# Two attention blocks with their rounds written out instead of looped, on all engines

## What is computed

```python
def reference(x, ctx_4096, mask_BxSxS2_ff1, ...):
    ...
    # _L0_attn_ref: q, k, v = x @ W.T + b, 32 heads of 16
    scores = jnp.where(causal, jnp.einsum('bhqd,bhkd->bhqk', q, k) / math.sqrt(hd), -jnp.inf)
    out = jnp.einsum('bhqk,bhkd->bhqd', jax.nn.softmax(scores, axis=-1), v)
    ...
    # _L0_xattn_ref: q from x, k and v from the context, q and k rotated (_rope), 4 query heads on each key head
    scores = jnp.einsum('bhgqd,bhkd->bhgqk', qg, k) / scale
    masked = jnp.where(mask[:, None, None].astype(bool), scores, -1000000000.0)
    out = jnp.einsum('bhgqk,bhkd->bhgqd', jax.nn.softmax(masked, axis=-1), v)
    ...
    x = _layernorm(x + _L0_attn_ref(...)); x = _layernorm(x + _L0_xattn_ref(...)); x = _layernorm(x + _L0_ffn_ref(...))
```

## Time and profile before

| | us |
|---|---|
| median of 3 runs | 1984.65 (1984.55 to 1985.22) |
| the profiled execution, whole | 1981.03 |
| its span in the profile | 1979.2 |
| PE busy | 1751.4 (88%) |
| DVE busy | 1353.7 (68%) |
| ACT busy | 940.9 (48%) |
| POOL busy | 936.9 (47%) |

### The profile page before, as it was taken

One profiled execution on the slowest core, in us unless ns is written; L12 is line 12 of the kernel. 1 busy time (PEld: TensorE's weight loads), 2 busy tenths in 40 slices (PEclk: granted clock), 3 DMA queues, 4 the chain that ended last, 5 costly groups with the idle time before them and its releaser, 6 DMA issues. The chain is left out here.

```text
span 1979.2 us, 45274 instructions
## 1 busy us (share of the span) xinstructions
PE 1751.4 (88%) x15496; PEld 1004.4 (51%) x15497; DVE 1353.7 (68%) x2069; ACT 940.9 (48%) x1565; POOL 936.9 (47%) x905
## 2 busy tenths in 40 slices
PE   6999999899999999999999999964678999999910
PEld 4666776555555555555555555533234554555500
DVE  5777888778788788887878888776753333333357
ACT  4556557654555654645545555434222333333334
POOL 6732024564554554645645546514344454445432
PEclk9999999999999999999999999986889999999965
DMA  9520011112221121221312203121313454643369
GB/s 265 124 44 24 3 56 50 54 65 76 75 90 61 65 97 54 97 78 41 118 44 85 86 33 118 65 72 54 106 64 129 141 205 168 220 151 111 111 235 311
DMA packets 82510, 200.13 MB, mean 101 GB/s; under 512 B 8704, under 2 KB 28544, under 8 KB 80320
## 3 DMA queue, kind: packets, MB, share of 16 engines
q1 hardware_dynamic: 63456, 136.89, 20.4%
q0 software_dynamic: 18912, 61.09, 9.9%
HBM read 141.86 MB, written 56.10 MB: 100 GB/s over the span
## 5 line engine op out<-in xcount | busy, mean ns | idle before, releaser
L382 PE MATMUL bank<-xhl,front_h 128*128 128x512 f16 x704 | 270.2, 384 | 20.5 <-DVEq L68 13.1
L383 PE MATMUL bank<-xhl,front_h 128*128 128x512 f16 x704 | 270.2, 384 | 0.0
L384 PE MATMUL bank<-xhl,front_l 128*128 128x512 f16 x704 | 269.9, 383 | 0.0
L1067 POOL TENSOR_TENSOR xa_xs<-xa_xs,sn 128x512 f32<-128x512 f32 x160 | 233.5, 1459 | 59.2 <-ACT xa_xs L1110 59.1
L1072 POOL TENSOR_TENSOR xa_rr<-xa_x,xa_xs 128x512 f32<-128x512 f32 x160 | 232.1, 1450 | 34.0 <-POOL xa_xs L1067 24.0
L1075 POOL TENSOR_TENSOR xa_sc<-xa_sc,xa_rs 128x1024 f32<-128x1024 f32 x32 | 62.2, 1945 | 374.2 <-DVE xa_rs L1281 374.2
L382 PE MATMUL bank<-out_h,xa_oh 128*128 128x512 f16 x512 | 194.2, 379 | 7.4 <-DVE xa_ol L1186 7.3
L383 PE MATMUL bank<-out_l,xa_oh 128*128 128x512 f16 x512 | 194.0, 379 | 0.0
L384 PE MATMUL bank<-out_h,xa_ol 128*128 128x512 f16 x512 | 194.0, 379 | 0.0
L1201 DVE TENSOR_TENSOR xa_x<-bank,cs 128x512 f32<-128x512 f32 x160 | 109.9, 688 | 84.7 <-ACT xa_xs L1110 82.5
L1109 ACT ACTIVATE xa_xs<-bank 64x512 f32<-64x512 f32 x160 | 95.0, 593 | 130.8 <-PE bank L384 127.2
(11 more groups left out here) (308 smaller groups left out, 4929.2 us busy)
## 6 DMA issues: line engine op xcount, KB each, us to landing
xa_rawc<-in_ew SPq DMA_DIRECT2D x33, 768.0 KB, 5.0
moe_ring<-scratch_w SPq DMA_DIRECT2D x16, 1536.0 KB
co_rows<-scratch_y SPq DMA_DIRECT2D x20, 1024.0 KB, 7.7
scratch_w<-xa_chunk_h SPq DMA_DIRECT2D x32, 384.0 KB, 2.3
scratch_w<-xa_chunk_l SPq DMA_DIRECT2D x32, 384.0 KB, 3.1
raw_front<-in_xwq SPq DMA_DIRECT2D x9, 1024.0 KB, 7.2
raw_out<-in_xwo SPq DMA_DIRECT2D x9, 1024.0 KB, 5.2
out<-raw_front SPq DMA_DIRECT2D x17, 256.0 KB, 6.7
```

The source lines that it names most:

```text
L382: pe.matmul(out_ap, ah, bh, start=start and m == 0, stop=False)
L383: pe.matmul(out_ap, ah, bl, start=False, stop=False)
L384: mm = pe.matmul(out_ap, al, bh, start=False, stop=stop and m == n - 1)
L1067: PO.mark(pool.tensor_tensor(xr, xr, sn[:, :].rearrange("p (a s) -> p a s", a=1) .to_broadcast([P, QT // S, S]), ALU.mult), f"sm{r}", st)
```

## The change

Every loop over rounds in `self_attention` and `cross_attention` becomes a Python `range`, on SP, ACT, DVE, PE and POOL. The round number is a constant everywhere, each instruction of each round stands in the program by itself, and no branch is left in the two blocks. What each step does and its order do not change: the steps of the round that was written out already keep their flag (`last`, `first`).

```diff
--- self_attention, sync
-                    with sp.Fori(0, NG - 1) as i:
+                    for i in range(NG - 1):
                         front_weights(i + 1)
--- self_attention, scalar, vector and tensor (the same on each)
-                    with act.Fori(0, NG - 1) as i:
+                    for i in range(NG):
                         for q in range(NQ):
-                            step(i, q)
-                    for q in range(NQ):
-                        step(NG - 1, q, True)
+                            step(i, q, i == NG - 1)
--- cross_attention, sync
-                    with sp.Fori(0, NG) as i:
+                    for i in range(NG):
                         nxt = (i + 1) % NG
--- cross_attention, gpsimd, scalar, vector and tensor (the same on each)
-                    for q in range(NQ):
-                        step(0, q, True)
-                    with pool.Fori(1, NG) as i:
+                    for i in range(NG):
                         for q in range(NQ):
-                            step(i, q)
+                            step(i, q, i == 0)
```

More of the change, by code:

```diff
@@ L791, in step @@
                             DV.mark(dve.scalar_tensor_tensor(wo_l, raw_o, WS, wo_h, ALU.mult, ALU.subtract), "wol", st)
-                    with dve.Fori(0, NG - 1) as i:
+                    for i in range(NG):
                         for q in range(NQ):
-                            step(i, q)
-                    for q in range(NQ):
-                        step(NG - 1, q, True)
+                            step(i, q, i == NG - 1)
                     done = Step(None, 0)
@@ L927, in step @@
                         back_out(st)
-                    with pe.Fori(0, NG - 1) as i:
+                    for i in range(NG):
                         for q in range(NQ):
-                            step(i, q)
-                    for q in range(NQ):
-                        step(NG - 1, q, True)
+                            step(i, q, i == NG - 1)
                     done = Step(None, 0)
@@ L1160, in step @@
                         AC.mark(act.activation(chunk_h[:, :], rawc[:, :], ACT.Copy, scale=WS), "ch", st)
-                    for q in range(NQ):
-                        step(0, q, True)
-                    with act.Fori(1, NG) as i:
+                    for i in range(NG):
                         for q in range(NQ):
-                            step(i, q)
+                            step(i, q, i == 0)
                     back_p(Step(None, 0))
@@ L1285, in step @@
                         DV.mark(dve.scalar_tensor_tensor(chunk_l[:, :], rawc[:, :], WS, chunk_h[:, :], ALU.mult, ALU.subtract), "cl", st)
-                    for q in range(NQ):
-                        step(0, q, True)
-                    with dve.Fori(1, NG) as i:
+                    for i in range(NG):
                         for q in range(NQ):
-                            step(i, q)
+                            step(i, q, i == 0)
                     st = Step(None, 0)
@@ L1385, in step @@
                             back_out(st, (2, 3))
-                    for q in range(NQ):
-                        step(0, q, True)
-                    with pe.Fori(1, NG) as i:
+                    for i in range(NG):
                         for q in range(NQ):
-                            step(i, q)
+                            step(i, q, i == 0)
                     st = Step(None, 0)
```

## The result

The changed kernel takes 1965.62 us (median of 6 runs, 1958.69 to 1968.51) beside 1984.54 us of the kernel before in the same session (6 runs, 1980.39 to 1985.22): a ratio of 0.9902, 95% interval 0.9881 to 0.9922, 18.9 us faster. A second timing gave 1965.3 beside 1984.06 us, 0.9907 (0.9889 to 0.9924).

A forecast was written before the change was run, and what follows sets the result against it. PE (TensorE) was taken to bound both blocks. Self-attention's 9.5 us (5.6 + 2.75 + 1.1) and cross-attention's 1.9 make 11.4 us, from a median of 1984.65 to 1973.2 us; range 1969 to 1979 us.

The forecast's parts named there:

- The bound, the branch, the stall: Both blocks: PE sets the pace; its taken branches back leave it idle, 5.6 us in self-attention and 3.9 at cross-attention's six edges.
- the edges: Passages from one looped round to the next: two in self-attention, six in cross-attention, the latter six predicted to give 1.7 us.
- The rival of the cheap branch: Both blocks: idle time is a wait for DVE and stays; only 1.1 us come back, 1983.5 us; chance 0.07.
- that of the fetches: DVE, ACT and POOL must fetch written-out code every round: 3.8 more blocks, 18.1 us cost, 1991.3 us; chance 0.04.
- the register instructions: Self-attention: constants instead of registers save 0.11 us in each of 10 looped steps, 1.1 us, between 0 and 2.5.
- what follows the stall: Self-attention: the steps behind the two edges are 2.2 and 0.55 us too long, from slow clock and restarting engines; 2.75 us.
- the rest of that row, seven waits of some 0.65 us, ... hangs on ACT and DVE, which are busy throughout, and stays: Cross-attention: PE's waits in each round's second step, behind the split of the output weights, were to gain nothing.
- what the gap loses, the sum itself gives back: Cross-attention, POOL: the 0.15 us shorter gap between product and sum leaves the period equal; the chain gains only 0.2 us.
- the lateness behind an edge: Cross-attention: DVE comes late into the next round, costing PE 0.56 us an edge without any branch, 0.36 after the change.
- the whole stall comes back: Both blocks: POOL's and DVE's chains shorten enough to return all stall time, 15.2 us, 1969.4 us; chance 0.12.
- DVE takes over: Both blocks: PE's gains beyond its own idle time are lost, the clock falls anyway; 6.1 us, 1978.5 us; chance 0.17.

## Why the prediction was right, and where it was wrong

**The bound, the branch, the stall: right.** PE sets the pace, the idle times at the edges are the branch's and not a wait for DVE. With PE looped they are there (2.86 and 2.97 us), without they are gone in every trace. The rival of the cheap branch falls. So does that of the fetches. It counted 3.8 blocks more, and there are 18 fetches more in q14; yet in the profiled execution PE has no idle time without a releaser in the blocks. Over the ten traces with self-attention written out on PE it has 0 to 1.6 us of it there, at no regular distance, against 0 to 1.05 us in the four with the loop.

**Self-attention, 9.5 us predicted, 9.2 measured as a mean and 9.6 in the profiled pair: the sum right, its split wrong.** The stall and what follows it were to give 8.35 us. PE's loop written out alone gives 5.7, or 7.3 without the idle times that nobody releases: the 5.6 of the stalls and the 1.7 of the clock. All engines but PE, on top of that, give 3.9 (183.07 - 179.14), or 2.3 without the same idle times, where the register instructions were to give 1.1. 7.3 and 2.3 are the pair's 9.6. Two errors cancelled.
- The term "what follows the stall" (2.75 us) was too large by 1.05. Of the steps behind the edges, 0.5 us each were put down to engines that start again in sequence; with the same stalls and those engines written out the steps take 17.89 and 17.88 us. The other 1.7 us, the clock's, came in three of four executions with these stalls, and at either edge; no run shows what decides it.
- The term "the register instructions" (1.1 us) was too small by 1.2. Its price of 0.11 us was taken from step (2, 3) alone; the steps (1, 0) and (1, 1) took 0.3 (the clock's 1.7 taken off) and 0.5 us longer than in the changed kernel. Only some 0.4 us of it were hidden by the stalls, in the two steps that end in one (with PE alone written out they take 18.22, without an idle time of 0.16, and 17.99 us, against 17.90).

**Cross-attention, 1.9 us predicted, 7.4 measured: wrong, and in two steps.** By step times the gain (7.6 us in the pair of profiled executions) consists of 3.4 us in seven second steps (30.86 to 30.38), 3.6 in the six last steps (182.3 in all, against 6 x 29.79 = 178.7), 0.3 behind the edges and 0.3 in step (1, 0).
- The step that failed first is "the rest of that row, seven waits of some 0.65 us, ... hangs on ACT and DVE, which are busy throughout, and stays". It was the largest row of the waits, and I set it aside from the names in it. ACT and DVE looped again cost 0.3 us; POOL looped again costs 5.4.
- The step behind it, which mis-sized the edges, is "what the gap loses, the sum itself gives back", from the equal periods of the earlier trace rows. They stand where the sum is contended, and the period there is still 2.90 us in the changed kernel. But the chain to PE goes through the sum's end, and in the chain's first rotations, where nothing contends, the period falls with the gap (1087.00 - 1084.42 = 2.58 us from sum to sum, against 1100.95 - 1098.23 = 2.72), the gaps add up, and DVE is held less long. So the lateness behind an edge did not go from 0.56 to 0.36 us; it went to nothing, and the full 3.9 us of the edges came back.

The rival "the whole stall comes back" had cross-attention's edges right and left out the second steps too; it got 4.35 us for the block. The range ended at 1969 because of it, so both the forecast and the range rested on the one sentence that the second steps stay. The rival "DVE takes over" has a true core: with PE alone written out DVE's lateness costs 0.49 us an edge. The change as made removes it, 0.36 us of it on POOL, as first steps of 30.15 us show with POOL alone looped.

**The rest.** Some 2 us of the measured gain lie outside the blocks, in stages that wander as much between executions of one kernel. They are left as chance; no run rules out a part of them.

## What to carry to other kernels

Time that is lost behind a stall need not be the stall's: put the stall back alone and look whether it returns. A small cost per step is to be read from all steps, not from the one that lies nearest to the control. Where two engines contend, equal periods say nothing; follow the end of the operation that the next engine is released by. And the largest row of waits on the bounding engine is to be traced to the engine that moves it, by its chain back, before it is said to stay.

## What the runs showed of the hardware

- An operation of DVE with two SBUF operands ended 0.54 to 0.55 us after the end of POOL's concurrent sum in four kernels, with durations of 0.76, 0.90, 1.04 and 1.04 us. Two gaps on POOL, each 0.14 us longer, became 0.28 us of DVE's duration.
- The busy time of DVE rose from 1353.7 to 1377.9 us with the same 2,069 operations. With POOL looped, or delayed by the small operation, it stays at 1354.1 and 1354.5. The group of the query's low parts in cross-attention shows it; before and after, from 449 to 1289 us:

```profile
L1206 DVE TENSOR_TENSOR xa_rql<-xa_rr,xa_rqh 128x512 f16<-128x512 f32 x110 | 97.5, 886 | 9.2 <-ACT xa_rqh L1116 7.5
```

```profile
L1196 DVE TENSOR_TENSOR xa_rql<-xa_rr,xa_rqh 128x512 f16<-128x512 f32 x112 | 129.1, 1153 | 7.5 <-ACT xa_rqh L1108 7.0
```

  The mean goes from 886 to 1153 ns while the block gets shorter: part of a busy time under contention is waiting, and less of it isn't by itself a gain.
- The register instructions between two dependent operations of POOL cost 0.14 us (0.22 against 0.08 us from product to sum).
- A branch back takes PE 4.2 to 4.8 us in self-attention's body of 1,200 matmuls and 3.3 to 3.9 in cross-attention's of 944. In a body of 112 in the same trace it takes 0.21 us; the branch rows of that one:

```profile
L1998 PEldq COMPARE_BRANCH  x20: 76/208/228, 1517.6 to 1886.8; - x20
```

- A stop of PE of 2.4 to 3.0 us is followed by 3.4 us at 1.2 GHz in some executions and by none in others, at the same place of the same code: three times at eight such stops, and never at that place in the ten executions without them.
